# First stage of an attention and expert kernel: one query product behind each tile's keys and values, in place of four at a group's end

## The reference, cut to what matters

```python
def _L0_attn_ref(X, ln_w, ln_b, W_in, b_in, W_out, b_out):
    h = _layernorm(X, ln_w, ln_b)
    qkv = h @ W_in + b_in
    Q, K, V = jnp.split(qkv, 3, axis=-1)
    Q = _rope_half(Q)
    K = _rope_half(K)
    A = jnp.sum(_cos_sim(K) * V, axis=-2)
    Y = A[:, None, :] * Q
    Y = Y @ W_out + b_out
    return Y + X
x = L0_attn_X                       # (2, 2048, 512), float32
x = x + _layernorm(_L0_attn_ref(_layernorm(x, axis=-1), ...), axis=-1)
x = x + _layernorm(_L0_ffn_ref(_layernorm(x, axis=-1), ...), axis=-1)   # 8 experts, top 2, and a shared one
return x
```

## Time and profile before

| | |
|---|---|
| median of 3 runs | 958.91 us (958.9 to 962.71) |
| profiled execution | 961.73 us, its span 959.9 us |
| PE, DVE, ACT, POOL busy in the span | 93%, 67%, 45%, 40% |
| first stage | from 15.6 us to 306.5 us |
| mean granted TensorE clock | 0.975 of full |

### The profile page before, as it was taken

The page is one execution under the profiler, slowest core; times in us unless marked ns, Lnnn a source line. Parts: engine busy times, 40 slices in busy tenths (PEclk is TensorE's granted clock), DMA queues, the critical chain, the costliest instruction groups (busy, mean ns, idle before and its releaser), DMA issues.

```text
span 959.9 us, 14789 instructions
## 1 busy us (share of the span) xinstructions
PE 888.0 (93%) x4558; PEld 729.5 (76%) x4558; DVE 642.1 (67%) x1378; ACT 436.2 (45%) x829; POOL 383.2 (40%) x313
## 2 busy tenths in 40 slices
PE   5999999999999799999999887899999999998885
PEld 4788777777888577777777676788888888886663
DVE  6866976966956655566566477465666656653778
ACT  5235445345253132241322445466666666664454
POOL 1456556456454000000000000568677776751262
PEclk9999999999999999999999898899999999999998
DMA  8327977977758975658422987589788878869998
GB/s 297 111 94 260 339 250 262 331 252 274 266 193 329 351 268 204 220 207 307 157 103 92 386 332 204 117 216 164 145 143 156 146 145 144 151 99 327 365 166 226
DMA packets 88683, 211.12 MB, mean 220 GB/s; under 512 B 11529, under 2 KB 19977, under 8 KB 83489
## 3 DMA queue, kind: packets, MB, share of 16 engines
q1 hardware_dynamic: 64128, 164.38, 47.4%
q0 software_dynamic: 18208, 41.50, 24.4%
q10 hardware_dynamic: 6272, 4.30, 1.6%
HBM read 119.14 MB, written 91.01 MB: 219 GB/s over the span
## 4 chain that ended last, share of the span: by engine, by line
PE 49%; DVE 11%; issue 6%; ACT 5%; POOL 3%; DMA 2%; DVEq 0%; POOLq 0%; ACTq 0%
PE bank L1565 5%; PE bank L1566 5%; PE bank L1567 5%; PE bank L1785 4%; PE bank L1783 3%; PE bank L1784 3%; PE bank L1770 3%; PE bank L1800 3%; PE bank L1802 3%; PE bank L1801 3%; PE bank L1792 2%; PE bank L1560 2%; ACT n L739 1%; DMA c_lo<-shared_scratch 1%; PE bank L1701 1%
## 5 line engine op out<-in xcount | busy, mean ns | idle before, releaser
L1514 POOL DMA_INDIRECT f_scratch<-ro,dst x71 | 112.5, 1585 | 53.4 <-SPq L582 24.3
L1506 POOL DMA_INDIRECT xr<-n_scratch,ids x71 | 70.2, 989 | 75.3 <-issue 53.9
L1565 PE MATMUL bank<-wkv_hi,h_hi 128*128 128x512 f32 x248 | 97.2, 392 | 0.0
L1567 PE MATMUL bank<-wkv_hi,h_lo 128*128 128x512 f32 x248 | 96.6, 389 | 0.0
L1566 PE MATMUL bank<-wkv_lo,h_hi 128*128 128x512 f32 x248 | 96.5, 389 | 0.0
L1306 DVE TENSOR_TENSOR ro<-bank,b2b 128x512 f32<-128x512 f32 x71 | 49.2, 692 | 65.9 <-PE bank L1802 55.8
L1783 PE MATMUL bank<-we,x_hi 128*128 x284 | 86.1, 303 | 0.2 <-DVE x_lo L1286 0.2
L1785 PE MATMUL bank<-we,x_lo 128*128 x284 | 80.5, 284 | 0.0
L1784 PE MATMUL bank<-we,x_hi 128*128 x284 | 80.4, 283 | 0.0
L632 ACT ACTIVATE sq<-kb 128x512 f32<-128x512 f32 x32 | 20.2, 632 | 125.9 <-DVE kb L941 125.9
L1483 POOL TENSOR_TENSOR zr<-zv,half 128x4 f32<-128x4 f32 x8 | 8.1, 1010 | 129.3 <-DVE zv L1074 129.3
(11 more groups left out here) (242 smaller groups left out, 2532.7 us busy)
## 6 DMA issues: line engine op xcount, KB each, us to landing
xg<-in_X SPq DMA_DIRECT2D x15, 1024.0 KB, 7.6
we<-expert_scratch SPq DMA_DIRECT2D x6, 2048.0 KB, 12.0
w_lo<-in_w SPq DMA_DIRECT2D x16, 512.0 KB, 5.6
expert_scratch<-w_hi SPq DMA_DIRECT2D x16, 512.0 KB, 3.0
expert_scratch<-w_lo SPq DMA_DIRECT2D x16, 512.0 KB, 4.1
q_scratch<-qh SPq DMA_DIRECT2D x8, 1024.0 KB, 3.9
q_scratch<-qb SPq DMA_DIRECT2D x8, 1024.0 KB, 6.2
q_hi<-q_scratch SPq DMA_DIRECT2D x8, 1024.0 KB, 4.8
```

The lines of the kernel that those rows point to most:

```text
L1506: pool.indirect_dma_start(xr[u][:, :], None, n3_dram, bass.IndirectOffsetOnAxis(ids[:, i:i + 1], 0)).then_inc(row_in[u], 16)
L1514: pool.indirect_dma_start(f_dram, bass.IndirectOffsetOnAxis(dst[:, i:i + 1], 0), ro[i % NRO][:, :], None, compute_op=ALU.add).then_inc(r_s ...
L1565: pe.matmul(dst, hi(k), w_hi(k), start=(k == 0), stop=False)
L1567: last = pe.matmul(dst, lo(k), w_hi(k), start=False, stop=(k == KD - 1 and not more))
```

## The change

From group 1 on, PE makes `q(g, j)` right behind `kv(g, j, 1)`; the first pair of turns stands in front of `q(g, 2)` and the second pair behind it. ACT takes the bias of a query product in each tile's turn and one unit's high part with each tile, and its `front_split` pairs stand behind `bias_q` of tile 2 and in front of that of tile 3. On POOL `q_times_sin` moves from behind `front_lo` to ahead of the last two `accumulate`. Group 0 stays as it was. DVE's and SP's orders are untouched.

```diff
                     if j == 1 and g >= 1:
                         q_hi_parts(g - 1)
-                    if j % 2 == 0:
-                        unit_hi_in(g, j // 2)
-                if g + 1 < NG:
-                    front_split(g + 1, (g + 1) % 2, (0, 1))
-                    bias_q(g, (0,))
-                    front_split(g + 1, (g + 1) % 2, (2, 3))
-                    bias_q(g, (1, 2, 3))
+                    unit_hi_in(g, j)
+                    if g >= 1:
+                        if j == 3 and g + 1 < NG:
+                            front_split(g + 1, (g + 1) % 2, (2, 3))
+                        bias_q(g, (j,))
+                        if j == 2 and g + 1 < NG:
+                            front_split(g + 1, (g + 1) % 2, (0, 1))
...
                 rnorm(g, 3)
+                if g >= 1:
+                    q_times_sin(g)
                 accumulate(g, 2)
                 accumulate(g, 3)
                 if g + 1 < NG:
                     front_lo(g + 1)
-                q_times_sin(g)
+                if g == 0:
+                    q_times_sin(g)
...
                 for j in range(GT):
                     kv(g, j, 0)
-                    if j == GT - 1 and g + 1 < NG:
+                    if g == 0 and j == GT - 1:
+                        turn(1, (0, 1))
+                    kv(g, j, 1)
+                    if g == 0:
+                        continue
+                    if j == 2 and g + 1 < NG:
                         turn(g + 1, (0, 1))
-                    kv(g, j, 1)
+                    q(g, j)
+                    if j == 2 and g + 1 < NG:
+                        turn(g + 1, (2, 3))
                 if g == 0:
+
                     pe.wait_ge(w_split, 3 * KD)
-                for m in range(KD):
-                    q(g, m)
-                    if m == 0 and g + 1 < NG:
-                        turn(g + 1, (2, 3))
+                    for m in range(KD):
+                        q(g, m)
+                        if m == 0:
+                            turn(1, (2, 3))
```

More of the change, by code:

```diff
@@ L646, in bias_q @@
                        .then_inc(q_free, 1)
-                    if m in (1, 2):
-                        unit_hi_in(g, 1 + m)
             def q_hi_parts(g):
@@ L700, in _ @@
                         q_hi_parts(g - 1)
-                    if j % 2 == 0:
-                        unit_hi_in(g, j // 2)
-                if g + 1 < NG:
-                    front_split(g + 1, (g + 1) % 2, (0, 1))
-                    bias_q(g, (0,))
-                    front_split(g + 1, (g + 1) % 2, (2, 3))
-                    bias_q(g, (1, 2, 3))
+                    unit_hi_in(g, j)
[6 more added lines that the diff above has]
+                if g == 0:
+                    front_split(1, 1, (0, 1))
+                    bias_q(0, (0,))
+                    front_split(1, 1, (2, 3))
+                    bias_q(0, (1, 2, 3))
                 if g == GB:
@@ L713, in _ @@
                     scale_wo(0)
-            act.wait_ge(tp_full, KD * NG)
-            bias_q(NG - 1)
             q_hi_parts(NG - 1)
```

## The result

The changed kernel takes **1057.7 us** (median of 4 runs, 1055.9 to 1062.1) against 960.2 us for the kernel before on the same chip: a ratio of 1.102, with a 95% interval of 1.098 to 1.106. That is 97.5 us more; forecast were 98. Its profiled execution took 1057.57 us with a span of 1055.8.

The account below looks back on a forecast made before the run. PE was taken to bound the stage, with six groups only 15.9 us above its own work. Terms -15.9 + 75 + 17.3 + 13 + 4 + 4.4 = +98 on 958.9 gave 1056.7, rounded to 1056 us; range 1024 to 1082.

Parts of the forecast that it names:

- old waits and slow starts gone: Groups 1 to 6: all PE time above its own work goes, -15.9 us.
- six waits in front of groups: In front of each of groups 2 to 7 PE waits 12.5 us for the last `h_lo`; +75 us (60 to 83).
- second pair of turns: Behind `q(g, 2)`, turns wait for ACT's bias and `hb`: 3.44 us in place of 0.56, six times, +17.3 us.
- clock at the groups' starts: Behind each of six long gaps PE's clock falls to 0.50; +13 us (6.5 if it recovers in half the time).
- clock at the turns: Waits at the second pair of turns lower PE's clock in half of the groups; +4 us (0 to 8).
- `sum_acc(1)`: At the stage's end PE waits for group 7's last `accumulate`; +4.4 us (3.8 to 5.6).
- The chain in front of PE: Last key tile to last `h_lo`, 12.84 us before, gains 2.42 from `rsn` on POOL; PE has 5.44 us to cover it.
- T + 17.9: Forecast end of POOL's last `h_lo`, counted from T, the end of the group's last key product.
- Contention: DVE instructions push in while POOL works off `acc` and `h_lo`: 2.4 us a group, between 0 and 3.8.
- The load behind the chain: Fourth unit's load ahead of ACT's second `front_split` pair puts the last `h_lo` at T + 15.9, hidden behind POOL: 0.

Follow-up runs that it names:

- e7: Changed kernel with `rsn` computed twice in the same place on GpSimd in groups 1 to 7; 1078.9 us.
- e1: Changed kernel with `rsn` on GpSimd put back behind the four `h_lo`; 1049.3 us.
- e6: Changed kernel with `rsn` back behind the four `h_lo` and the fourth unit's high part behind the second `front_split` pair; 1038.9 us.
- e9: Changed kernel's one query product per tile in groups 1 to 6, turns between second and third query product, splits earlier, group 7's four at its end; 961.6 us.
- e11: Changed kernel's one query product per tile and turns in groups 1 to 6, `front_split` and `h_lo` earlier, group 7's four query products at its end; 957.7 us.
- e4: Changed kernel with VectorE waiting for the next group's last `h_split` before `unit_lo(g, 2)` and `rotate_q` in groups 1 to 6; 1049.5 us.
- e5: Changed kernel with the fourth unit's high part behind the second `front_split` pair on ScalarE; 1057.4 us.
- e2: Changed kernel with the first `front_split` pair on ScalarE ahead of the third query product's bias; 1044.6 us.
- e3: Changed kernel with 46 extra matmuls in front of the wait for `h_split` of groups 2 to 7; 1049.2 us.
- e12: Kernel before, four query products still at the group's end, with earlier splits and second pair of turns, first pair at its old place; 953.9 us.
- e8: Changed kernel with the first `front_split` pair ahead of the third bias and 46 filler matmuls in front of groups 2 to 7; 1031.7 us.

## Why the prediction was right

The forecast and what the runs showed, term by term:

| term | forecast us | measured us |
|---|---|---|
| old waits and slow starts gone | -15.9 | about -11 (the rest of the sum) |
| six waits in front of groups | +75 | +70.2 |
| second pair of turns | +17.3 | +15.7 |
| clock at the groups' starts | +13 | +14.9 |
| clock at the turns | +4 | 0 |
| `sum_acc(1)` | +4.4 | +4.5 |
| stage, and behind it | +98 | +94.5, and 1.3 |

The waits are counted here as in the prediction, from one start to the next less 0.227 us (104.74 - 92.44 - 0.23 = 12.07 in front of group 2); the list of waits, which counts from the listed end of a matmul, has 0.16 less for each. The two lines of PE:

```profile
92.44 0.39 PE L1571 MATMUL bank<-h_hi,wq_lo 128*128 128x512 f32 x1
104.74 0.79 PE L1569 MATMUL bank<-wkv_hi,h_hi 128*128 128x512 f32 x1 [11.92 <-POOL h_lo L1430]
```

And the matmul of the kernel before that stands ahead of the turns of the earlier trace rows:

```profile
257.57 0.39 PE L1567 MATMUL bank<-wkv_hi,h_lo 128*128 128x512 f32 x1
```

- The chain in front of PE: shown by e7, which lengthened it and the waits alike, and by e1 with e6, which shortened both; e9 and e11 took it away from there. The forecast T + 17.9 was T + 17.46.
- Contention was put at 2.4 us a group; 17.21 - 12.84 - 2.42 = 1.95 us was measured, and e4 took 1.6 to 2.0 away. The Trainium skill (GPSIMD Engine Reference, section 8, Key points) names this contention without a price; in these runs it lengthens instructions of both engines and lies on the path.
- The load behind the chain: right by e5, and e1 with e6 show it as the next limit. I had worked out where it lies but not said that a single repair would meet it.
- The turns: (84.39 - 80.75) - 0.23 = 3.41 us from the end of the third query product to the next key product in group 1, forecast 3.44. Above the cost of a pair without a wait, 0.80, that is 2.61 us, 15.7 in six groups; e2 got 13.8 back.
- The clock: the price at the groups' starts was near, 14.9 for 13. At the turns nothing was paid in the profiled execution; e3, e4, e5, e6 and e7 paid there in one to six groups with the same two waits, so that was luck. Not foreseen was that it fell behind the wait of 4.3 us at `sum_acc(1)` too, where it stood at 0.51 until 407.9. What that costs isn't told: what follows the stage is 1.3 us longer than before, but it varies from 652.5 to 659.0 us over the profiled executions.
- The mis-sized term is the first, because a pair of turns was taken too cheap. The prediction has 258.60 - 257.81 - 0.227 = 0.56 us, but between these two starts there are transposes alone. Counted from the matmul ahead of them it is 258.60 - 257.57 - 0.227 = 0.80 us, and all twelve pairs of e12, none of which waits, cost just that. So a group that never waits takes 34.2 us, not 33.8, `sum_acc(0)` takes PE another 0.8 (201.67 to 202.48 in the kernel before), and of the 15.9 us only 12.2 could be won; about 11 of them were.
- The errors of the terms, +5, -4.8, -1.6, +1.9, -4 and +0.1, sum to -3.3: they cancel in good part, so the sum is nearer than its parts, and that is luck.

## What to carry to other kernels

Work that is spread evenly covers less than the same work in one block: before moving products forward, count how long the chain behind the last input of a round is and what is left to cover it. Where one engine serves several chains, put what the next round needs ahead of what this round's end produces; here that was worth 93 to 99 us of the stage in the interleaved order (e9 and e11, whose turns and last group changed with it) and 0.8% in the old one. After one repair look for the second limit close behind, and count the loss of clock with the gap that makes it.

## What the runs showed of the hardware

- VectorE and GpSimd instructions that meet stand still for one another by turns, also when both have a queue: `w_lo` and `rc` 2.28 us each in place of 1.22, two `acc` 3.91 in place of 2.6, four `h_lo` 6.82 in place of 5.2 (the changed kernel, end of group 2).
- Filling a gap of 12 us with matmuls kept the granted clock at 1.00 there, and a restart lost 0.14 us in place of 2.5 (e8 and e3 against the changed kernel).
- Waits of 1.54 and 0.67 us around a pair of turns brought the clock to 0.50 in group 1 of e3 and of e7 and left it at 1.00 in the changed kernel, with the same instructions of PE around them. Which waits bring it down thus isn't told by their length alone, and a forecast has to carry both cases.
